# Layer 2's attention over the context moved into the bank-7 plan of its heads, and layer 1's feed-forward started with two tiles beside the heads' end

## The reference, cut to what matters

```
x  -> layer 1: attention with 16 heads of 16, then attention over ctx with 16 heads (int8 rows)
x  -> layer 1: x += bitlinear(gelu(bitlinear(ln(x), w1, b1)), w2, b2)         # 256 -> 1024 -> 256
x  -> layer 2: attention with 32 heads of 8, causal, 8 key/value heads
x  -> layer 2: x += softmax(ln(x) @ ctx^T / 16, masked) @ ctx * valid         # one head, per batch
x  -> layer 2: 8 experts, top 2
```

## Time and profile before

| | |
|---|---|
| runs shown | 2354.26, 2355.17 and 2366.03 us, median 2355.17 |
| the profiled execution, its own time | 2366.2 us |
| its span from first to last instruction | 2364.2 us, 38315 instructions |
| mean granted TensorE clock | 0.922 of 2.4 GHz |
| busy share of the span | PE 85%, DVE 66%, ACT 49%, POOL 36% |

### The profile page before, as it was taken

One profiled execution on the slowest core, in us unless ns is written; L12 is line 12 of the kernel. 1 busy time (PEld: TensorE's weight loads), 2 busy tenths in 40 slices (PEclk: granted clock), 3 DMA queues, 4 the chain that ended last, 5 costly groups with the idle time before them and its releaser, 6 DMA issues.

```text
span 2364.2 us, 38315 instructions
## 1 busy us (share of the span) xinstructions
PE 2013.3 (85%) x13443; PEld 1456.4 (62%) x13521; DVE 1570.7 (66%) x4123; ACT 1152.7 (49%) x2563; POOL 855.5 (36%) x1374
## 2 busy tenths in 40 slices
PE   5999967899985799955698999589999999997991
PEld 4888844566652456532255667368788787774670
DVE  4876657456668456546577979578888888765433
ACT  1347647334438344426557646155555655552330
POOL 3248751112123111110000000166766767764445
PEclk9999978999996699975699999799999999998996
DMA  6114430000000300010000000411111111135543
GB/s 262 44 66 145 146 127 1 1 2 2 2 30 0 148 8 2 2 38 1 0 1 1 1 1 1 158 41 41 49 51 46 41 41 46 45 104 161 122 134 104
DMA packets 57693, 130.96 MB, mean 55 GB/s; under 512 B 6656, under 2 KB 23552, under 8 KB 55520
## 3 DMA queue, kind: packets, MB, share of 16 engines
q1 hardware_dynamic: 52656, 115.80, 14.3%
q0 software_dynamic: 4560, 12.46, 2.5%
q10 hardware_dynamic: 288, 0.26, 0.0%
HBM read 100.31 MB, written 26.08 MB: 53 GB/s over the span
## 4 chain that ended last, share of the span: by engine, by line
PE 69%; DVE 13%; ACT 7%; issue 4%; POOL 4%; DMA 1%; SPq 1%; POOLq 0%; another core or an unknown queue 0%; DVEq 0%; ACTq 0%
PE ps L1072 4%; PE ps L2690 4%; PE ps L2349 4%; PE ps L2368 4%; PE ps L2712 3%; PE ps L2736 3%; PE ps L1112 3%; PE ps L3144 3%; PE ps L1092 3%; PE ps L1139 2%; PE ps L2744 2%; PE ps L2681 2%; PE ps L2672 2%; PE ps L2673 2%; PE ps L601 2%
## 5 line engine op out<-in xcount | busy, mean ns | idle before, releaser
L3000 POOL TENSOR_TENSOR K<-K 128x512 f32<-128x512 f32 x128 | 144.8, 1131 | 146.8 <-DVE K L2797 146.8
L2397 DVE TENSOR_TENSOR_SCAN W<-W,ps 128x512 f32<-128x512 f32 x128 | 155.8, 1218 | 40.1 <-issue 24.6
L1305 ACT ACTIVATE K<-ps 128x768 f32<-128x768 f32 (+1 forms) x128 | 110.7, 865 | 146.2 <-PE ps L1112 144.5
L2349 PEld LDWEIGHTS ps<-K 128*128 128x128 f32 x1024 | 136.6, 196 | 65.0 <-issue 50.6
L2940 ACT ACTIVATE K<-ps,K 128x256 f32<-128x256 f32 x128 | 60.8, 475 | 213.8 <-DVE K L2781 213.8
L2792 DVE TENSOR_SCALAR K<-ps,K 128x128 f32<-128x128 f32 x384 | 131.0, 404 | 27.5 <-POOL K L3017 27.1
L2349 PE MATMUL ps<-K 128*128 128x128 f32 x1024 | 139.2, 280 | 6.8 <-DVE W L2397 6.8
L2986 POOL TENSOR_SCALAR K<-K 128x1 f32<-128x1 f32 x16 | 3.6, 224 | 371.3 <-DVE K L2847 368.9
L237 POOL TENSOR_SCALAR Z<-Z 128x1 f32<-128x1 f32 x80 | 19.9, 248 | 321.6 <-DVE Z L232 321.6
L2368 PE MATMUL ps<-W,C 128*128 128x512 f32 x256 | 132.2, 598 | 0.7 <-DVE W L2405 0.6
L2690 PE MATMUL ps<-K 128*128 128x256 f32 x512 | 131.8, 380 | 0.7 <-ACT K L2959 0.7
(11 more groups left out here) (523 smaller groups left out, 5748.1 us busy)
## 6 DMA issues: line engine op xcount, KB each, us to landing
W<-split_weights SPq DMA_DIRECT2D x32, 768.0 KB, 4.3
split_weights<-W SPq DMA_DIRECT2D x40, 384.0 KB, 2.6
W<-in_m SPq DMA_DIRECT2D x32, 256.0 KB, 4.8
results<-K SPq DMA_DIRECT2D x63, 128.0 KB
W<-split_weights SPq DMA_DIRECT2D x1, 5376.0 KB, 16.6
W<-in_wproj SPq DMA_DIRECT2D x16, 256.0 KB, 3.1
W<-in_m SPq DMA_DIRECT2D x32, 128.0 KB, 5.1
W<-split_weights SPq DMA_DIRECT2D x1, 3072.0 KB, 21.0
```

What stands on the lines that cost most here:

```text
L1305: e.activation(to, made, ACT.Exp, scale=self.SCALE).then_inc(*self.up("exp"))
L2349: m = e.matmul(ps[1 + 2 * (n % 2)][:, b * 128:(b + 1) * 128], self.dtuT[h][:, i, b * 128:(b + 1) * 128], self.diag[s % 4][:, b * 128:(b + ...
L2397: e.tensor_tensor_scan(self.st[i % 3], self.a[i % 3], ps[1 + 2 * (i % 2)][:, :], 0.0, ALU.mult, ALU.add).then_inc(*sig.up("m scan"))
L3000: e.tensor_tensor(Pv, Pv, st[:, 4:6].unsqueeze(2).to_broadcast([128, 2, 256]), ALU.mult).then_inc(*sig.up("x scaled"))
```

## The change

`L2Cross` as a stage is gone. Its work is now four kinds of entry in `L2Attn`'s bank-7 plan for each of the 8 tiles: "look" (scores, mask, maximum), "mix" (transposes of the exponentials), "gain" (product with ctx, sum into x, statistics) and "last norm". They lie 3, 8, 10 and 19 quarters behind the tile's "norm", whose quarters are 53, 57, 85, 89, 117, 121, 149 and 153. The exponential follows a look by two quarters. The context, its transpose and the mask are loaded by `L2Attn.sp`, ahead of the experts' weights; the load of `kv_parts` (3072 KB) moves to the start of `L3Attn`.

`L1Ffn` no longer starts a tile with each step: the starts are `FROM`, and the first two tiles use banks 5 and 6, which the heads' units have left by q = 103. The other six use banks 2, 3, 4 and 7. Steps 0 to 11 (tiles 0 and 1) follow quarters 104 to 126; tiles 2 to 5 start at steps 12 to 15 (q = 128 to 133), tiles 6 and 7 at steps 19 and 20, behind the heads' last quarter. `L2Attn` begins at step 15, two quarters to a step, up to q = -2; from q = -1 it runs after step 31. The rest of the diff gives `L1Heads` and `L2Attn` room in memory and passes `self.bank(...)` where a bank's number stood.

```diff
 class L1Ffn:
+    PHASES, FIRST = 14, 2
+    FROM = (0, 2, 12, 13, 14, 15, 19, 20)
-    STEPS = NT + PHASES - 1
+    STEPS = FROM[-1] + PHASES - 2
     def tiles(self, step):
-        return [(t, step - t) for t in range(max(0, step - self.PHASES + 1), min(NT, step + 1))]
+        return [(t, step - self.FROM[t]) for t in range(NT) if 0 <= step - self.FROM[t] < self.PHASES]
+    def bank(self, tile, n):
+        return self.ps[((5, 6, 5, 6, 5, 6) if tile < self.FIRST else (4, 2, 3, 7, 4, 7))[n]]
...
 class L2Attn(SmallHeads):
+    def more(self, b, end):
+        at = []
+        for i in range(2):
+            q = 4 * (end + 5 + i) + 1
+            at += [(q + 3, "look", 2 * b + i, 0), (q + 8, "mix", 2 * b + i, 0), (q + 10, "gain", 2 * b + i, 0),
+                   (q + 19, "last norm", 2 * b + i, 0)]
+        return at
+    def more_pe(self, t, kind, n, bank):
...
+        if kind == "look":
+            t.wait_ge(self.sig["l2c ctxT"], 16)
+            t.wait_ge(self.sig[nx.name + " xnT"], nx.tbase + n + 1)
+            for k in range(2):
+                m = e.matmul(bank[:, 0:256], nx.xnT[:, k, n * 128:(n + 1) * 128], self.cT[:, k, n // 2 * 256:n // 2 * 256 + 256],
+                             start=k == 0, stop=k == 1)
+        elif kind == "mix":
+            t.wait_ge(self.s("looked"), n + 1)
+            for k in range(2):
+                m = e.transpose(bank[:, k * 128:(k + 1) * 128], self.P[n % 2][:, k * 128:(k + 1) * 128], self.g.ident)
...
 class Layers:
-    EARLY = {124: 0, 126: 1, 129: 2, 132: 3, 136: 4, 140: 5, 145: 6}
-    BESIDE, CROSS = 12, 18
+    EARLY = {104: 0, 106: 1, 108: 2, 110: 3, 112: 4, 114: 5, 116: 6, 118: 7, 120: 8, 122: 9, 124: 10, 126: 11, 128: 12,
+             130: 13, 131: 14, 133: 15, 136: 16, 139: 17, 143: 18}
+    BESIDE, CROSS = 15, 18
...
         for q in front[3 * (self.cross.STEPS - self.CROSS):]:
             yield "heads", q
             if q in self.EARLY:
-                yield "ffn", self.EARLY[q]
...
+                yield from self.beside(self.EARLY[q], behind)
+        for step in range(max(self.EARLY.values()) + 1, self.ffn.STEPS):
+            yield from self.beside(step, behind)
+        for q in behind:
             yield "attn", q
+    def beside(self, step, behind):
+        yield "ffn", step
+        for n in range(2):
+            if step >= self.BESIDE and behind[0] < -1:
+                yield "attn", behind.pop(0)
...
-class L2Cross:
...
-STAGES = [(1, L0Attn), (7, Layers), (8, L2Cross), (9, L2Moe),
+STAGES = [(1, L0Attn), (8, Layers), (9, L2Moe),
```

More of the change, by code:

```diff
@@ L1545, in pe_at @@
     def pe_at(self, t, step):
[L1546 removed]
+        g, sig, e, h, nx = self.g, self.sig, t.e, self.heads, self.g.norms[6]
         for i, ph in self.tiles(step):
+            if ph in (2, 3, 6, 7, 11) and i < self.FIRST:
+                for u in range(len(h.last) - 2, len(h.last)):
+                    h.wait_part(t, u, h.last[u])
+                t.wait_ge(sig["l1f kept"], self.reached(2, step - 1))
+                t.wait_ge(sig["l1f biased"], 2 * self.reached(3, step - 1))
+                t.wait_ge(sig["l1f hidden kept"], self.reached(6, step - 1))
+                t.wait_ge(sig["l1f x"], self.reached(7, step - 1))
+                t.wait_ge(sig[nx.name + " xnT"], nx.tbase + self.reached(11, step - 1))
             if ph == 2:
@@ L1721, in sp, with more @@
-        d.e.dma_start(self.g.kv_parts, self.g.parts[16:24].rearrange("b p n -> p b n")).then_inc(*self.sig.up("w kv parts", 16))
+    def more(self, b, end):
+        at = []
[5 more added lines that the diff above has]
+    def more_pe(self, t, kind, n, bank):
+        e, nx = t.e, self.g.norms[7]
+        if kind == "look":
[8 more added lines that the diff above has]
+                m = e.transpose(bank[:, k * 128:(k + 1) * 128], self.P[n % 2][:, k * 128:(k + 1) * 128], self.g.ident)
+        elif kind == "gain":
+            t.wait_ge(self.sig["l2c ctx"], 16)
+            t.wait_ge(self.s("kept"), self.number["mix", n, 0] + 1)
+            for k in range(2):
+                m = e.matmul(bank[:, 0:256], self.cTurned[n % 2][:, k, :], self.ctx[:, n // 2 * 2 + k, :], start=k == 0, stop=k == 1)
+        else:
+            self.g.norms[8].turn(t, n, bank)
+            return None
+        return m
@@ new lines, in more_act @@
+    def more_act(self, a, kind, n):
+        e, nx = a.e, self.g.norms[8]
+        if kind == "mix":
+            a.wait_ge(self.s("rest"), self.made_rest[kind, n, 0])
+            e.activation(self.cTurned[n % 2], self.ps[7][:, 0:256].rearrange("p (k n) -> p k n", k=2),
+                         ACT.Copy).then_inc(*self.up("kept"))
+        elif kind == "last norm":
+            nx.keep(a, n, self.ps[7])
+            a.wait_ge(self.sig[nx.name + " xnT"], nx.tbase + n + 1)
+            e.nop().then_inc(*self.up("kept"))
@@ L1795, in order @@
                     yield "heads", q
+        behind = [q for q in self.attn.quarters]
         for q in front[3 * (self.cross.STEPS - self.CROSS):]:
```

283 lines of the change are left out of this document (132 added, 151 removed).

## The result

The change makes the kernel slower. The median is 2396.77 us (2390.78 to 2397.45, 4 runs) against 2360.60 us (2354.26 to 2366.77, 4 runs) of before: ratio 1.0148, 95% interval 1.0109 to 1.0187. The profiled execution took 2390.78 us, its span is 2388.8 us with 38328 instructions, and the granted TensorE clock is 0.913. The medians differ by 36.2 us, the two profiled spans by 24.6: the profiled execution is the fastest of its four here, and that of before took 2366.2 us, near the slowest of its four.

A forecast was written before the change was run, and what follows sets the result against it. PE was taken to bound layer 2's heads, a chain over three engines the feed-forward's stretch. Terms -2.5 + 27 + 5 - 11 = +18.5 us took the median 2355.2 to 2373; 8-in-10 range 2336 to 2396.

The forecast's parts named there:

- beside the heads: Layer 1's heads, q = 105 to 127: feed-forward steps 1, 3, 5 and 7 hold back exponentials, +27 us (+6 to +35).
- behind q = 128: From there to layer 2's q = -1: two tiles' DVE work leaves, 106.2 us becomes 95, -11 us (-46 to 0).
- part one: The context's attention as pieces in layer 2's heads and tail: 13.3 + 5 - 20.8 = -2.5 us (-17 to +2).
- Layer 2's heads +13.3: Looks, mixes, gains and last norms up to quarter 128 add 14.8 us of PE work, 1.5 taken as covered.
- The tail +5 and -20.8: Bank-7 tail: entries ahead of serial turns, +5 us; behind tile 6's norm 18.3 us in place of 39.1, -20.8.
- +5 for the clock: Layer 1's heads: waits of 6, 10 and 5 us put PE at 1.2 GHz oftener, +5 us (0 to +20).
- step 1: Feed-forward step at q = 106, rows of tile 0: 5.7 us to PE's next probabilities, 3.2 as it was, 2.5 more.
- step 3: Feed-forward step at q = 110, tile 0's Gelu and tile 1's rows: 10.1 us, before 3.3, so 6.8 more.
- my walk: Behind q = 128, steps 12 to 31 walked through with listed durations: 48, 45 and 6 us, 99 in all; 95 taken.
- The faster one: Rival: three engines interlock well behind q = 128, that stretch shrinks to 72 us, total 2341 us; chance 0.26.
- The slower one: Rival: layer 1's heads fall to 1.2 GHz, clock +20 instead of +5, +34 in all, 2389 us; chance 0.14.
- Smaller stalls beside the heads: Rival: blocks beside the heads cost 15 instead of 27, the stretch behind takes 90, total 2354 us; chance 0.22.

The follow-up runs named there:

- pool_later: The changed kernel with POOL's parts of the maxima issued two quarters later, for both layers' heads: 66.3 us from q = 105 to 127, ratio 1.0138.
- delay_only: The kernel before, with unread copies on ACT ahead of four exponentials of layer 1's heads: 60.1 us from q = 105 to 127, ratio 1.0116.
- delay_filled: The kernel before, with unread ACT copies ahead of four exponentials and unread PE products in the time opened: 56.4 us from q = 105 to 127, ratio 1.0080.
- late_starts: The changed kernel with feed-forward starts at steps 0, 2 to 8 and the old quarters (124 on), keeping new banks and pieces: 2386.32 us, ratio 1.0098.
- tail_filled_5: Context attention as pieces, feed-forward as before, plus 5 unread PE products behind each bank-7 entry from q = 129: 2355.19 us, ratio 0.9970 to the kernel before.
- pieces_only: The changed kernel with the feed-forward put back as before, so only the context's attention is in pieces: 2364.75 us, ratio 1.0002 to the kernel before.
- tail_filled: Context attention as pieces, feed-forward as before plus waits, 12 unread PE products behind each bank-7 entry from q = 129: 2365.76 us, ratio 1.0021 to the kernel before.

## Why the prediction was right in its direction and short in size

**Direction and sum.** I had forecast slower as the likeliest sign (0.49), +18.5 us. The stretches say +30.2, and the ratio times the median that I started from gives 2390, inside 2336 to 2396. The median of the change's own runs, 2396.77, is 0.8 us above that range. Of the 11.7 us between +18.5 and +30.2, 8.2 were missed beside the heads and 4.3 behind q = 128, and part one was 0.8 better than forecast. That +18.5 was for a profiled execution; the medians say +36.2, about twice as much, and no window shows where the other 6 us lie. Of the signs named, six table loads in place of two up to layer 2's heads are there (the first at 676.68, the last at 839.73), and the exponentials spread over 74.5 us, not 60.

**Part one: right.** Layer 2's heads +13.3, measured +14.7. The tail +5 and -20.8, measured -18.1 together; from tile 6's kept norm to the last kept turn I had 18.3 us and the trace has 17.5 (1064.79 to 1082.31). Sum -2.5, measured -3.3; run alone, no measurable difference. The two parts of the tail, -15.8 in sum, were measured only together. Of its steps one was taken as given and isn't: the tail's low clock, which 5 unread products lift, for 7.6 to 8.1 us.

**Beside the heads: the step that failed.** I had +27 and +5 for the clock; stretch 1 grew by 40.2. The missing 8.2 us are POOL's queue: the prediction wrote "1.3 + a copy 0.4 + 1.7 ..." for step 1 and let DVE's rows start when DVE was free. It never asked where the deviation that they need stands in POOL's order, so that wait was put at nothing. With POOL's parts moved, stretch 1 grows by 32.0, and the four gaps between exponentials can be set beside mine:

| gap ahead of the exponential behind step | before | predicted | after | pool_later |
|---|---|---|---|---|
| 1 | 3.1 | 5.7 | 9.6 | 5.9 |
| 3 | 3.8 | 10.1 | 12.8 | 12.2 |
| 5 | 2.6 | 13.5 | 18.6 | 15.4 |
| 7 | 2.6 | 9.4 | 10.8 | 10.8 |

The prediction had 3.2, 3.3, 2.0 and 3.0 for the first column, 0.6 us less in sum. By the table the four gaps grow by 39.7 us in the kernel after, nearly all of the 40.2.

That pool_later's 32.0 is just +27 and +5 is in part luck: the forecast had a row for the lower level, but none for how much of it reaches the path. The remaining 5.6 us of pool_later over the forecast (44.3 against 38.7) are about as much as that term. At step 3, for one, the lower level is on the path:

```profile
668.95 1.13 PE L1177 MATMUL ps<-W,K 128*128 128x256 f32 x4
...
674.46 1.46 PE L1103 MATMUL ps<-K 32*128 32x256 bf16 x12
...
675.85 2.07 PE L1177 MATMUL ps<-W,K 128*128 128x256 f32 x4
...
677.96 0.42 DVE L1220 TENSOR_TENSOR X<-ps,X 128x256 f32<-128x256 f32 x1 [0.77 <-PE ps L1177]
...
681.28 0.83 PE L1103 MATMUL ps<-K 32*128 32x256 bf16 x12
```

The scores take 1.46 us where they take 0.83 later in the same gap, and DVE waits 0.77 us for a product of 2.07 us that takes 1.13 at the upper level: some 1.4 of this gap's 2.1 us over the forecast. delay_only and delay_filled give the clock 3.7 us where the delays are pure. The table loads were right at 1.3 each.

**Behind q = 128: right in sign, short.** -11 forecast, -6.7 measured at these cuts. Cut where the prediction cut, at the four products at 810.77 before (L1151) and 836.57 after (L1162), the stretch is 99.0 us, the 99 of my walk; I had moved away from it to 95 on DVE's share, without a row for it. late_starts shows that the new banks and their waits can cost: 17.5 us against the old plan with the old starts. How much of that the change itself pays stays open.

**The rivals.** The faster one (the stretch behind at 72 us, from 77 on) fell: 103. The slower one had the right size, +34. Its condition came true, with the clock at 0.63 in stretch 1, but not its price of +20: with the clock low, pool_later grows by 32.0, where +20 for the clock beside the blocks' +27 would be 47; what took the kernel after to 40.2 is POOL's queue. Smaller stalls beside the heads fell: 40, not 15.

## What to carry to other kernels

When a step is moved between two others, write down for every engine what stands ahead of each of its instructions in the new place, for the helper engine with its 0.2 us instructions too: what it queues behind may itself wait for something that comes half a step later. Two waits in one place should also be removed together before they are given up: apart they gave 8.2 and 11.1 us here, together 24.8. And in a serial tail at the low clock, a few products that end within a handover that exists anyway can pay (7.6 to 8.1 us here, where the rearrangement gave 3.3 net); count them so that they don't reach the next entry, and don't expect it where PE isn't in the chain.

## What the runs showed of the hardware that I had not expected

The same instructions drew different clocks. tail_filled_5 has the instructions of pieces_only all through stretch 1, and took 32.9 us at 1.00 where that took 34.5 at 0.95. tail_filled differs in it only by waits behind q = 124, and took 39.0 at 0.81; it had already lost 1.1 us between the exponentials of q = 119 and 121 (4.15 against 3.06), ahead of these waits. Stretch 3 took 212.8 us at 0.92 in tail_filled and 204.3 at 0.97 in pieces_only, with the same products. Windows of stretches 1 and 3 of tail_filled, the second with 198.06 us of PE where pieces_only has 189.48:

```profile
663.70:702.67 38.97, 33.95 (x366) 19.50 (x364) 21.41 (x54) 12.67 (x15) 9.19 (x33) 0.81 0.08 30
```

```profile
815.54:1028.36 212.82, 198.06 (x2074) 119.88 (x2087) 123.45 (x277) 82.65 (x135) 37.24 (x170) 0.92 0.06 23
```

late_starts has the same 212.8 with the same 198.06 of PE. The place is the same in both, and in pool_later too: counted from the first exponential of layer 2's heads, these three agree with the kernel after within 0.4 us up to the exponential of q = 105, are 6.8 to 6.9 us behind it at q = 113 and 8.3 at q = 121. The same eight products in pool_later and in the kernel after, 9.16 us apart in their traces as all rows of the 3 us ahead of them are, to 0.02 us:

```profile
1008.30 0.81 PE L1123 MATMUL ps<-K 32*128 32x256 bf16 x8
```

```profile
1017.46 0.50 PE L1123 MATMUL ps<-K 32*128 32x256 bf16 x8
```

In pool_later PE is at the lower level from here to about 1025 (the granted clock is 0.50 from 1015 to 1025 and 0.98 in the ten us behind), in the kernel after at the upper one. What decides it stays open. So neither late_starts's 8.5 us nor 8.3 of pool_later's 11 can be put on their edits. Stretches 1 and 3 of a single profile are therefore good to about 6 and 9 us where the clock in them differs, and to a few tenths where it doesn't. Stretch 1's readings above rest on the gaps in which a wait was seen to go, not on the totals alone. Stretch 4 lies within 0.3 us in all seven kernels that have the new plan and no fillers.
